# Two-layer sequence model on one core: the attention's value products moved ahead of both transposes of their step

## What is computed

```python
x = rmsnorm(tokens, norm_w)
q = x @ Wq
k, v = split(x @ Wkv, 2)
sim = einsum('bhid,bhjd->bhij', q, k) * SCALE
sim = where(causal_mask, -max, sim)
attn = softmax(sim)
out = einsum('bhij,bhjd->bhid', attn, v)
out = sigmoid(x @ Wg) * out
return out @ Wout
```

## Time and profile before

| | |
|---|---|
| median of 3 runs | 1357.38 us (1356.96 to 1359.4) |
| the profiled execution | 1357.57 us, its span 1355.8 us |
| busy over the span: PE, DVE, ACT, POOL | 94%, 67%, 47%, 43% |
| attention, from the first scores to the last value products | about 829.8 to 1188.9 us of the span |
| mean granted TensorE clock | 0.976 |

### The profile page before, as it was taken

The page is one execution under the profiler, slowest core; times in us unless marked ns, Lnnn a source line. Parts: engine busy times, 40 slices in busy tenths (PEclk is TensorE's granted clock), DMA queues, the critical chain, the costliest instruction groups (busy, mean ns, idle before and its releaser), DMA issues. The chain is left out here.

```text
span 1355.8 us, 22860 instructions
## 1 busy us (share of the span) xinstructions
PE 1277.2 (94%) x7798; PEld 709.1 (52%) x7798; DVE 908.5 (67%) x1773; ACT 638.1 (47%) x1537; POOL 588.2 (43%) x939
## 2 busy tenths in 40 slices
PE   7999677999999999998899998999999999899999
PEld 4443224566566566555445454555555556454545
DVE  6999996888988998989301206788787787530100
ACT  3266213555555565565322315566565665622221
POOL 2632315787888878888200002444344353410000
PEclk7999888999999999999899999999999999899999
DMA  2368896555555555556100002000000000000000
GB/s 81 155 256 339 317 391 218 192 183 183 187 188 184 183 185 190 185 183 235 63 0 0 0 1 88 1 1 1 1 1 1 1 1 1 1 1 0 16 0 15
DMA packets 67714, 143.51 MB, mean 106 GB/s; under 512 B 6800, under 2 KB 22800, under 8 KB 64784
## 3 DMA queue, kind: packets, MB, share of 16 engines
q1 hardware_dynamic: 62992, 129.47, 27.0%
q10 hardware_dynamic: 4608, 12.58, 2.3%
HBM read 94.58 MB, written 47.45 MB: 105 GB/s over the span
## 5 line engine op out<-in xcount | busy, mean ns | idle before, releaser
L1775 POOL TENSOR_SCALAR pr<-pr,rs,sg 128x512 f32<-128x512 f32 (+3 forms) x256 | 151.8, 607 | 209.4 <-DVE rs L1677 209.4
L615 PE MATMUL banks<-w_bc,valueT 128*128 128x512 f32 x448 | 212.0, 597 | 3.9 <-ACT own L909 3.1
L974 DVE TENSOR_TENSOR pp<-banks,rec 128x1024 f32<-128x1024 f32 x128 | 156.1, 1220 | 9.4 <-DMA dd<-det 3.3
L1588 ACT ACTIVATE pr<-banks,nm 128x512 f32<-128x512 f32 (+3 forms) x256 | 132.5, 523 | 24.9 <-DVE nm L1671 22.1
L615 PEld LDWEIGHTS banks<-w_bc,valueT 128*128 128x128 f32 x448 | 77.3, 192 | 61.4 <-issue 60.4
L1671 DVE TENSOR_REDUCE nm<-banks 128x2 f32<-128x1024 f32 (+3 forms) x128 | 105.5, 824 | 4.4
L1576 ACT COPY prT<-banks 128x512 f32<-128x512 f32 (+3 forms) x128 | 54.2, 424 | 112.0 <-PE banks L1472 111.8
L1056 POOL TENSOR_SCALAR_AFFINE_SELECT bp<-bp 128x1024 f32<-128x1024 f32 x64 | 73.5, 1148 | 76.4 <-ACT bp L863 76.3
L1312 DVE TENSOR_TENSOR x<-x,banks 128x256 f32<-128x256 f32 x16 | 6.7, 421 | 148.3 <-PE banks L1223 148.3
L856 ACT COPY qk<-banks 128x512 f32<-128x512 f32 x128 | 74.9, 585 | 64.2 <-PE banks L743 64.2
L1472 PE MATMUL banks<-ident,pr 128*128 128x128 f32 x640 | 98.7, 285 | 5.3 <-ACT prT L1576 4.1
(11 more groups left out here) (239 smaller groups left out, 2422.2 us busy)
## 6 DMA issues: line engine op xcount, KB each, us to landing
rec<-psi SPq DMA_DIRECT2D x128, 512.0 KB, 4.4
psi<-X SPq DMA_DIRECT2D x15, 2048.0 KB, 7.3
det<-w_bc ACTq DMA_DIRECT2D x16, 512.0 KB, 4.6
dd<-det SPq DMA_DIRECT2D x64, 128.0 KB, 4.7
bcs<-pre ACTq DMA_DIRECT2D x16, 256.0 KB, 6.8
w_bc<-in_w_bc SPq DMA_DIRECT2D x4, 1024.0 KB, 10.8
back<-bcs SPq DMA_DIRECT2D x16, 256.0 KB, 4.9
w_bc<-in_f_h SPq DMA_DIRECT2D x4, 1024.0 KB, 7.7
```

The costliest lines, as they stand in the source:

```text
L615: mm = pe.matmul(bank, m["valueT"][:, c, t * P:(t + 1) * P], w, start=(c == 0), stop=(c == 1))
L974: dve.tensor_tensor(pp[:, q % 2].rearrange("p (a c) n -> p a c n", c=2), sc.unsqueeze(2).broadcast_to([P, 4, 2, HN]), rec[:, n % RL, q % 2 ...
L1588: act.activation(pr[:, n % RP, h, 0:w], S[n % 2][:, h, 0:w], ACT.Exp, bias=nm[:, n % 4, h:h + 1], accum_out=sm[:, m % 3, n % 2, h:h + 1]). ...
L1775: pool.tensor_scalar(row, row, rs[:, n // 2 % 2, n % 2, h:h + 1], sg[:, TPB * b + it, hd:hd + 1], ALU.mult, ALU.mult).then_inc(s["scaled"], 1)
```

## The change

In an even step, `values(g-2)` moves from between the two turns to directly behind the two scores, so that both turns stand behind it. Only TensorE's program changes. No instruction is added or taken away, and the other engines' programs stay as they are.

```diff
@@ -1526,6 +1526,8 @@
                 if m < COUPLES:
                     scores(2 * m)
                     scores(2 * m + 1)
+                if not odd and g >= 2:
+                    values(g - 2)
                 if m == 0:
                     turn_rows(2)
                     turn_rows(3)
@@ -1539,8 +1541,6 @@
                     if outs_done(g) > 0:
                         pe.wait_ge(s["added"], outs_done(g))
                     project_q(g + 2)
-                if not odd and g >= 2:
-                    values(g - 2)
                 if LAG <= m < COUPLES + LAG:
                     turn(2 * (m - LAG) + 1)
                 if not odd and b + 1 < B:
```

## The result

The changed kernel takes 1394.6 us (median of 4, 1393.32 to 1397.67) against 1357.74 for the kernel before: a ratio of 1.0278, 95% interval 1.0257 to 1.0298. It is slower by 36.9 us; the forecast was 1397.2 us, 39.6 more. The profiled execution of the changed kernel took 1397.67 us with a span of 1395.9. From the first scores to the start of the closing run of four project_out it has 397.6 us (832.11 to 1229.71), the kernel before 359.8 (829.77 to 1189.60): 37.8 us of the 40.1 by which the spans differ lie in this stretch. The other 2.3 lie mostly ahead of it, in stages that the change does not touch, and come and go between executions (the stretch starts at 827 to 838 us in the profiles of this study).

What follows compares the result with a forecast made beforehand. TensorE's program order was taken to bound the attention. Losses over the pairs of groups 2 to 31, step 64's turns and the first late take_k summed to 39.6 us, giving 1397.2 us; terms' range 1390 to 1406, with rivals 1380 to 1418.

Steps and rivals of the forecast that it cites:

- The second turn loses its cover: Even steps, counted from V, the value products' start: second turn waits for first turn's copies; next scores at V + 5.34.
- TensorE's own loss: TensorE's added wait at the second turn: 0.79 us in each pair of steps, between 0.60 and 1.16.
- The chains and take_k: Late copies delay ScalarE, VectorE and take_k, then the next value products: pairs without project_out 11.43 against 10.08, +1.35 us.
- Last sequence: Groups 24 to 31, no value chunk: next scores wait for exponentials; +1.56 us a pair with project_out, +1.78 without.
- The sum: Attention pairs 18.9, 6.3, 6.2 and 7.1, step 64's turns 0.8, first late take_k 0.3: together 39.6 us.
- step 2's excess: Step 2, without value products between its turns, takes 3.42 us against 2.25; 1.16 taken as upper bound of TensorE's loss.
- Rival 1: Attention pairs: only TensorE's own wait counts, ScalarE catches up; 31 x 0.79 = 24.5 us, 1382; chance 0.15.
- Rival 2: Attention pairs: waits add up in a longer chain; 31 x 1.72 = 53 us, 1411 and some more; chance 0.12.
- Rival 3: Attention: granted clock falls; 55 us on top, 1452, or 14 in the last eight pairs, 1411; large case 0.05.
- Rivals 4 and 5: Attention: faster, value products covering first-turn waits, at best 1352, chance 0.04; or nothing measurable, 1357.4, chance 0.04.
- rival 4: Before the first turn: value products cover its waits, at most 5.3 us gained, 1352; waits at start and end; 0.04.
- The bank rule: Transposes' banks 4 and 5, now used twice running: rotation advice speaks against the change; alone it gives 24.5 us, 1382.

Runs made afterwards that it cites:

- e2: Against the changed kernel, the value products moved behind both back-to-back turns, ahead of the value chunk; 1398.45 us, ratio 1.0310 to the kernel before.
- e3: The changed kernel with VectorE's copy of a group's first turn (128x512 out of bank 5) made twice; 1421.78 us, ratio 1.0480 to the kernel before.
- e4: The kernel before the change with VectorE's copy of a group's first turn made twice; ratio 1.0019 to the kernel before, 2.8 us more.
- e5: The changed kernel with banks exchanged: value products to bank 7, value chunk to bank 6; 1388.5 us, ratio 1.0228 to the kernel before.
- e1: The changed kernel with the value chunk moved between the two turns of its even step; 1391.71 us, ratio 1.0265 to the kernel before.

## Why the prediction was right

*Direction and bound.* That TensorE's order bounds the attention, and that what counts is the cover between the turns, holds: e2, e3 and e4 show it from three sides.

*The second turn loses its cover.* Predicted: VectorE's copy at V + 3.42, head 1 at V + 4.24, the next scores at V + 5.34. Measured: 3.51, 4.35 and 5.44. TensorE's own loss was put at 0.79 us; by the scores it is 0.89, and in the pairs with project_out the window shows 0.95 (13.33 - 12.38), for there the chunk's slot is 0.07 longer as well (e5). The term undersized is the time to the copy's start; I had scaled it from a turn of six transposes. The 8 pairs cost 8.1 us, where 6.3 were forecast: the first in each sequence loses 1.2.

*The chains and take_k.* Predicted mask V + 6.56, last exponential V + 10.56, next V at 11.43; measured 6.40, 10.41 and 11.26. The links are the ones named; the string on VectorE, from its copy to the mask, was put at 3.14 us and takes 2.89, 0.25 less, for I took the small copy at its duration (0.28) where its slot is 0.20, and take_v and invert (0.86, measured 0.69) from a place with a wait in it. With the copy's start 0.09 later than forecast, the mask is 0.16 early. 14 pairs should have cost 18.9 us; their windows add up to 16.0.

*Last sequence.* Predicted windows 11.0 and 13.1, measured 10.97 and 12.97. The scores start at V + 5.04 (1155.08 to 1160.12), by the exponentials, as forecast (5.16). There too a copy was taken at its duration (0.58) where its slot is 0.48 (1158.14 to 1158.62), and the 0.10 from the exponentials' end to the scores, for which the forecast showed no row, is 0.05.

*The sum.* Forecast 39.6; 37.8 in the profiles' stretch and 36.9 between the medians. By parts, 18.9 became 16.0, 6.3 became 8.1, and the rest (14.4: the last sequence, step 64 and the first take_k) 13.7. The undersized and the oversized terms partly cancel, and that the sum lies within 2 us owes something to luck. One slip has no effect: step 2's excess is 3.42 - 2.25 = 1.17, not 1.16.

*The rivals.* Rival 1 (1382) falls by the windows (11.26, not 10.9) and by e5, which gives 0.31 of a pair to take_k, a link that TensorE's own wait does not contain. Rival 2 (the longer chain) falls by the windows. Rival 3: the clock kept 1.00 in the repeating steps; its falls in steps 4 and 5 and behind step 62 are in the kernel before as well. Rivals 4 and 5 fall by the result. The waits that rival 4 counted on are where it was said: one group's value products at the attention's end start behind 3.14 us of idle time in the changed kernel, and their place gains nothing.

*Signs that were wrong.* I wrote that take_values would come earlier than VectorE's copy of 512. It comes behind it (916.89 against 915.49), because VectorE's program has it there; my own list of what is queued behind that copy said so. The slip did not enter the sum, but it hid what e1 then showed: take_values in that place is part of the string that sets the pair. I had also given the second turn's idle time to VectorE's copy alone. Of its 0.64 us ScalarE's copy ends 0.38, ahead of head 0, and VectorE's 0.26; on the page ScalarE's copy ends 12.5 of the 22.3 us. And head 1 starts 2.04 us behind the first turn, not 1.9.

*The bank rule.* What the Trainium skill says (Perfetto Trace Analysis, section Matmuls), that groups should rotate through the banks so that draining overlaps, is borne out in its direction by e2 and e3. By itself it would have given the first rival's time. Of a pair without project_out, which loses 1.18 us, TensorE's own wait is 0.89 (the scores at V + 5.44 for T + 4.55), and the chains behind it are the rest; in the last sequence, where the pair loses 1.75, they are more.

## What to carry to other kernels

Where two products use the same PSUM bank in turn, what stands between them is not free to move: ask how long the copy out of the bank takes from the first one's start, and whether something as long stays between. When such a copy becomes late, follow the program order of the engine that makes it; what is queued there (here take_values, maxima and exponentials, and take_k at the end) can set the time even after the first wait is covered. Doubling the suspected copy in both orders tells at once which of them covers it. Where the granted clock differs between profiles, compare repeating windows at the same clock rather than whole stretches.

## What was not expected

The cover removed was worth more than the idle time of the line that it covered: TensorE's waits ahead of the transposes grew by 17.0 us, the stretch by 37.8. Two chains that end within some hundredths of a microsecond of each other (6.40 and 6.41 in the changed kernel) make an experiment on one of them (e1) show nearly nothing; only the removal of both tells.

In e3 the granted clock fell in the last sequence, behind a pair in which TensorE was busy for 9.79 of 11.79 us; later pairs, busy for 11.79 of 13.71, kept 1.00. The windows are of that pair, of the fall, and of a later pair:

```profile
1131.64:1143.43 11.79, 9.79 (x58) 5.36 (x57) 8.86 (x18) 6.39 (x23) 4.75 (x8) 1.00 0.01 2
...
1171.69:1185.40 13.71, 11.79 (x75) 7.03 (x74) 8.96 (x18) 7.08 (x25) 4.75 (x8) 1.00 0.00 0
```

```profile
1151.00:1156.00 5.00, 4.60 (x19) 2.89 (x18) 3.74 (x9) 2.48 (x11) 2.37 (x4) 0.66 0.00 0
```

The last row is the fall; 0.66 is a mixture of the two levels, 1.2 and 2.4 GHz. The pair in which it began took 13.31 us where 11.7 were due (10.96 and the 0.73 of the second copy), 1.6 more, near the 1.76 that rival 3 had reckoned; the next pair had a mean clock of 0.89 and took 14.95, where 13.9 were due (13.17 in the changed kernel and 0.73). Such a fall is not e3's alone. In the kernel before it lies in steps 4 and 5, behind a pair in which TensorE was busy for 9.96 of 11.15 us, and e3 has none there. Why it comes where it does stays open.
